# Decoder layer (linear mixer, cross-attention, expert-choice FFN) on one core: struck-out logits in PSUM, regrouped weight loads in the last batch, a ninth ring slot, first expert ahead of the bias work

## What is computed

```python
x = x + mixer(layernorm(x))                      # linear attention with running sums
Q = layernorm(x) @ Wq.T; K, V = ctx @ Wkv.T      # ctx: (16, 750, 256), 16 heads of 32
x = x + softmax(Q K^T * scale) V @ Wo.T
# expert-choice FFN on xn = layernorm(x): 32 experts, each takes its best 8 tokens of 224
logits = xn @ gate_w.T + gate_b
probs = softmax(logits, axis=tokens)
vals, idx = top_k(probs per expert, 8)
merged = sum_k vals[k] * xn[idx[k]]              # one row per sequence and expert
h = gelu([merged, 1] @ w1[e]);  o = [h, 1] @ w2[e]
x = x + scatter_add(idx, o * vals)
```

## Time and profile before

| what | us |
|---|---|
| median of 3 runs | 2262.58 (2260.3 to 2263.67) |
| the profiled execution, its own time | 2257.76 |
| its span, first to last instruction | 2256.1 |
| attention stage ends, expert stage begins | about 1577 of the span |
| PE busy over the span | 1858.3 (82%) |
| DVE busy | 1028.3 (46%) |
| POOL busy | 823.6 (37%) |
| chain of work that ended last: transfers into the ring | 22% of the span |

### The profile page before, as it was taken

The page is one execution under the profiler, slowest core; times in us unless marked ns, Lnnn a source line. Parts: engine busy times, 40 slices in busy tenths (PEclk is TensorE's granted clock), DMA queues, the critical chain, the costliest instruction groups (busy, mean ns, idle before and its releaser), DMA issues. The chain is left out here.

```text
span 2256.1 us, 41492 instructions
## 1 busy us (share of the span) xinstructions
PE 1858.3 (82%) x12594; PEld 1211.7 (54%) x12594; DVE 1028.3 (46%) x2541; ACT 745.9 (33%) x1551; POOL 823.6 (37%) x591
## 2 busy tenths in 40 slices
PE   7889999999999999999999999976756656556544
PEld 5667777677677776777777777753211111111111
DVE  1355766667667666666676666642100000000003
ACT  3144444445445444454454543532100000000000
POOL 0255555545555555465555555543000000000000
PEclk9799999999999999999999999977878787787776
DMA  5324333333243243332432433364899999999996
GB/s 172 88 67 109 78 77 95 82 87 95 74 106 77 76 97 81 89 96 74 103 78 76 99 80 82 80 223 146 367 418 421 421 420 423 422 420 421 422 377 252
DMA packets 143265, 421.34 MB, mean 187 GB/s; under 512 B 33036, under 2 KB 79084, under 8 KB 118652
## 3 DMA queue, kind: packets, MB, share of 16 engines
q1 hardware_dynamic: 135580, 411.70, 53.4%
q10 hardware_dynamic: 6656, 8.15, 1.0%
q0 software_dynamic: 992, 1.02, 0.1%
HBM read 307.37 MB, written 17.14 MB: 144 GB/s over the span
## 5 line engine op out<-in xcount | busy, mean ns | idle before, releaser
L1139 DVE TENSOR_REDUCE maxes<-bank 112x1 f32<-112x376 f32 (+1 forms) x1024 | 511.1, 537 | 129.6 <-PE bank L1345 127.0
L943 ACT ACTIVATE probs<-bank 125x448 f32<-125x448 f32 x768 | 399.5, 546 | 156.9 <-PE bank L1367 150.0
L1367 PE MATMUL bank<-q_st,k_st 98*125 98x224 f32 x1536 | 338.6, 307 | 23.5 <-DMA q_st<-max_lo 21.9
L821 POOL TENSOR_TENSOR psum_keys<-psum_keys,probs 125x896 f32<-125x896 f32 x127 | 266.6, 2099 | 214.9 <-ACT probs L943 209.8
L1345 PE MATMUL bank<-k_st,q_st 96*112 96x376 f32 (+1 forms) x1024 | 319.6, 358 | 21.5 <-DVE maxes L1139 18.9
L1753 PE MATMUL bank<-ring,hid_T 128*32 128x512 f32 x1024 | 175.5, 848 | 194.2 <-DMA ring<-in_L_ffn_w 191.0
L1367 PEld LDWEIGHTS bank<-q_st,k_st 98*125 98x125 f32 x1536 | 258.3, 192 | 82.2 <-issue 48.1
L1671 DVE TENSOR_TENSOR o_fin<-bank,b_row 16x512 f32<-16x512 f32 x32 | 21.7, 679 | 586.0 <-PE bank L1711 586.0
L824 POOL TENSOR_TENSOR psum_keys<-psum_keys,probs 125x896 f32<-125x896 f32 x127 | 266.7, 2100 | 9.9
L1593 POOL DMA_DIRECT2D o_rows<-o_fin x31 | 15.2, 492 | 597.7 <-DVE o_fin L1671 597.7
L1345 PEld LDWEIGHTS bank<-k_st,q_st 96*112 96x112 f32 x1024 | 170.2, 181 | 77.9 <-DVE maxes L1139 50.3
(11 more groups left out here) (168 smaller groups left out, 2762.4 us busy)
## 6 DMA issues: line engine op xcount, KB each, us to landing
ring<-in_L_ffn_w SPq DMA_DIRECT2D x128, 2048.0 KB, 30.4
k_st<-k_hi SPq DMA_DIRECT2D x512, 93.8 KB, 2.1
k_st<-k_lo SPq DMA_DIRECT2D x256, 93.8 KB, 2.2
q_st<-q_hi SPq DMA_DIRECT2D x504, 28.0 KB, 1.8
ctx_nat<-in_ctx SPq DMA_DIRECT2D x16, 750.0 KB
x_in<-in_x SPq DMA_DIRECT2D x16, 448.0 KB, 3.7
out<-x SPq DMA_DIRECT2D x16, 448.0 KB, 3.1
out<-ring ACTq DMA_DIRECT2D x28, 256.0 KB, 3.0
```

Source lines behind the costliest of these rows:

```text
L821: nc.gpsimd.tensor_tensor(psum_keys[:], psum_keys[:], lo, ALU.add).then_inc(pool_chain, 1)
L943: nc.scalar.activation(probs[n % 2][:, j, :], bank[5 + u % 2][0:SK, 0:2 * T], ACT.Exp, scale=SCALE).then_inc(probs_ready, 1)
L1139: nc.vector.tensor_reduce(maxes[:, j, t, c:c + 1], score_bank(n)[0:TT, 0:SC[c + 1] - SC[c]], AX.X, ALU.max).then_inc(s_drained, 1)
L1367: last = nc.tensor.matmul(bank[5 + u % 2][0:SK, kk * T:(kk + 1) * T], k_st[slot][:, j, k * SK:(k + 1) * SK], q_st[slot][:, j, :], start=Tr ...
```

## The change

- `beaten` lies in PSUM, in the unused half of the bank that holds the gate logits of that batch. `z_mix` is left to the mixer.
- The ring has nine places. Four tensors that were elsewhere (`wv_lo`, `ctx_lo`, `xh`, `bias_row`) and a rest now fill the place of the ninth, number 4 (`EXTRA`); the former slots 4 to 7 sit one place further (`home_of`). After the mixer's last use, chunk 0 of expert 2 is loaded into it once and read from there by `expert(1, 0, False, EXTRA)`; the first round of reloads leaves that chunk out. The expert loops start at 2, with round 1 written out.
- In the last batch the eight first chunks are released at the start of a group: each group's first `scores_T` must be done, then chunks 0, 1, 2 (group 0), 3, 4 (group 1), 5 and the extra one (group 2), 6 (group 3), and 7 after the last scores. `store` now comes behind the first three; `keep_weight` and `keep_routed` come behind chunk 6.
- `tok` is cleared at the start of the attention stage. The first expert's w1 matmuls come before PE's transposes of the bias rows, and DVE does both `take` of round 0 before `adder` and `b1_T`.

```diff
+        EXTRA = 4
+        def home_of(slot):
+            return slot if slot < EXTRA else slot + 1
...
-        wv_lo = sb(es, "wv_lo", [P, KC, D], F32R)
-            bias_row = sb(es, "bias_row", [TT, D])
+        tok = sb(es, "tok", [P, 2, KD, 32])
...
+        wv_lo = inside("wv_lo", P, [KC, D], F32R)
+        ctx_lo = inside("ctx_lo", P, [KC, S], F32R)
+        xh = inside("xh", TT, [2, D])
+        bias_row = inside("bias_row", TT, [D])
         end_slot()
...
-        ring = sb(es, "ring", [P, SLOTS, 2 * H])
+        ring = sb(es, "ring", [P, SLOTS + 1, 2 * H])
...
+                def extra_weight():
+                    sp.wait_ge(yt_ready, 2 * B)
+                    sp.wait_ge(x_bias_ready, B)
+                    sp.wait_ge(chunk_in[0], 16)
+                    load_chunk(sp, 2, 0, None, 0)
+                def last_batch_weights(kt):
+                    if kt == 0:
+                        sp.wait_ge(x1_ready, 2 * B)
+                        first_weights([0])
+                        sp.wait_ge(v_ready, NK * B)
+                        sp.wait_ge(q_ready, 4 * B)
+                        sp.wait_ge(k_ready, 8 * B)
+                        first_weights([1, 2])
+                    elif kt == 1:
+                        sp.wait_ge(q_stacked[3], 192 * B)
+                        sp.wait_ge(k_stacked[3], 192 * B)
+                        first_weights([3, 4])
+                    elif kt == 2:
+                        first_weights([5])
+                        extra_weight()
+                    else:
+                        first_weights([6])
...
+                        if kind == "last":
+                            sp.wait_ge(scores_ready, (LAST * 4 + kt) * 12 + 1)
+                            last_batch_weights(kt)
                         if kt == 3 and kind != "first":
                             keep_weight(b - 1)
...
                     nc.gpsimd.memset(weight[:], 0.0).then_inc(constants, 1)
+                    nc.gpsimd.memset(tok[:], 0.0).then_inc(cleared, 1)
...
+                def beaten(kind):
+                    return bank_of("gate", kind)[0:E, T:2 * T]
...
-                    nc.vector.match_replace(beaten[:], top8[:], logits[:], NEG
+                    nc.vector.match_replace(beaten(kind), top8[:], logits[:], NEG
                                             ).then_inc(router_chain, 1)
...
-                    nc.vector.scalar_tensor_tensor(out=weight[0:E, :], in0=beaten[:], scalar=NEG,
+                    nc.vector.scalar_tensor_tensor(out=weight[0:E, :], in0=beaten(kind), scalar=NEG,
...
-                with sp.Fori(1, E // 2 - 1) as i:
+                weights(1, 0, False, (1, 2, 3))
+                weights(1, 1, False)
+                with sp.Fori(2, E // 2 - 1) as i:
...
+                        slot = home_of(slot)
+                        if extra is not None and kd < 2:
+                            slot = extra
...
                     last.then_inc(h_full, 1)
+                    if first and e2 == 0:
+                        flip_biases()
...
                 expert(0, 0, True)
                 expert(0, 1, True)
-                with pe.Fori(1, E // 2) as i:
+                expert(1, 0, False, EXTRA)
+                expert(1, 1, False)
+                with pe.Fori(2, E // 2) as i:
```

More of the change, by code:

```diff
@@ L109, in build @@
     assert N_MID % 2 == 0
+    assert all(q.index("wt0") - q.index("gate") <= 2 for q in (SEQ["mid"], SEQ["last"], SEQ["tail"]))
     def place(job, kind):
@@ L1674, in _ @@
                 take(0, 0, True)
+                take(0, 1, True)
+                for c in range(HC):
+                    part = slice(c * 32, (c + 1) * 32)
+                    nc.vector.tensor_copy(adder[part, :], ident[part, part]
+                                          ).then_inc(adder_ready, 1)
+                dve.wait_ge(b1_flipped, 1)
+                nc.vector.tensor_copy(b1_T[:].rearrange("p t c e -> p (t c e)"), bank[4][:]
+                                      ).then_inc(b1_ready, 1)
                 add_biases(0, 0, True)
-                take(0, 1, True)
                 row_out(0, 0, True)
```

74 lines of the change are left out of this document (26 added, 48 removed).

## The result

The changed kernel takes 2235.72 us (median of 4 runs, 2233.17 to 2237.96), the kernel before beside it 2262.26: ratio 0.9883, interval 0.9866 to 0.99. It is faster by 26.5 us; I had said 16.4, and a time of 2246.2 in a range from 2237. Timed again in another comparison it was 2240.91 against 2258.9, ratio 0.9922 (0.9904 to 0.9939), 18.0 us. Its profiled execution took 2234.32 us (span 2232.7), 23.4 us less than that of before.

A forecast was written before the change was run, and what follows sets the result against it. Weight stream bounds the expert stage; in attention PE is fullest, and its last-ending waits matter. Gains 9.4 + 1.4 + 1.0 + 4.6 = 16.4 us take the profiled 2257.76 to 2241.4; adding 4.8 gives 2246.2, range 2237 to 2257.

The forecast's parts named there:

- Struck-out logits in PSUM: Router's third group: instruction shortens to 0.39 us, wait at wt0 goes; 0.67 us a batch, 9.4 us over fourteen middle batches.
- that now hangs on the PE score matmul of 532.51: Router's third group: q_lo waits on this matmul through DVE's preceding maximum, so wt1 moves only from 534.17 to 533.50.
- the bound of 1.5 us a batch: Middle batches: upper bound of the PSUM edit's gain, all of what DVE gains; lower bound nothing.
- Rival 1: Middle batches: another wait fills the gap at wt0, or PSUM does not free the instruction; 2257.0 us, chance 0.12.
- rival 4: Router: striking out into PSUM is much slower; at 1.90 us an instruction the kernel takes 2269.3 us, chance 0.03.
- Last batch: Last attention batch: 1.4 us gained from the PSUM edit and 1.0 us from the release by groups.
- rivals 2 and 3: Last batch: max rows come out between chunks, 2238.5 us, chance 0.12; or wait for everything issued before, 2252.2, chance 0.10.
- they land 1 us earlier: Last batch: with the store behind the first chunks, max rows still wait about one chunk but land 1 us earlier.
- Ninth slot and first expert: Expert stage: one chunk of 5.0 us fewer, PE starts 1.8 us earlier, stream gap of 2.2 us; gain 4.6 us.
- the port rule: Expert stage start: whichever POOL instruction or two-port DVE copy starts first holds shared ports throughout; sum 0.4 us smaller.
- the first term: Middle batches: gain from striking out logits into PSUM, 0.67 us a batch, 9.4 us.
- the third term: Expert stage: gain from the ninth slot and the earlier first expert, 4.6 us, bounds 3 and 7.5.

The follow-up runs named there:

- run 1: Kernel before with only the struck-out logits moved to PSUM; 18.5 us faster than the kernel before, ratio 0.9915.
- run 3: Changed kernel with the last batch's chunks issued at the places of the kernel before; 2242.44 us.
- run 6: Changed kernel, but each last-batch group's chunks are issued only after that group's max rows have landed; 10.4 us faster than the changed kernel beside it.
- run 7: Changed kernel with the last store and the recall of routed rows issued ahead of chunk 7; 5.9 us faster than the changed kernel.
- run 11: Changed kernel with max rows ahead of the weights, last store ahead of chunk 7 and picks cleared late; 2226.32 us.
- runs 6 and 12: The second of these: run 11 plus a second chunk issued to fill the expert stage's stream gap, against the changed kernel; 2223.23 us.

## Why the prediction was right and wrong

*Struck-out logits in PSUM.* That PSUM frees the instruction, and that PE's wait at wt0 goes with it, was right; what PE waits for next was wrong, and so the term was too small, 0.67 us a batch where 13 of the 14 batches gave 1.2: 9.4 us forecast, 14.9 measured, 14.3 alone. The step that failed is "that now hangs on the PE score matmul of 532.51, since DVE must first take the maximum of the one before it". These rows of before show what VectorE did behind the long instruction:

```profile
530.19 0.36 PE L1345 MATMUL bank<-k_st,q_st 96*112 96x376 f32 x1
...
532.81 0.53 DVE L1139 TENSOR_REDUCE maxes<-bank 112x1 f32<-112x376 f32 x1
```

The maximum of 532.81 was for the score matmul of 530.19, over since 530.55; it stood late only because VectorE was held. I tied it to the matmul just ahead of it in time, when it read an older one. In the changed kernel it runs at 529.42, more than 1 us ahead of the last score matmul, and q_lo no longer hangs on it: wt1's 0.29 us went as well. I had the bound of 1.5 us a batch on paper and took the nearest row's wait as the value; a count of maxima against score matmuls would have told. (A smaller slip: the earlier trace rows show 67 to 109 GB/s in slices 2 to 26, not 66 to 109 everywhere before the last quarter; nothing hung on it.) Rival 1 (the gap is filled) fell, and so did rival 4: 0.372 us into PSUM against 0.364, as small as taken.

*Last batch.* 2.4 us forecast (1.4 + 1.0), 5.4 measured, 4.6 over all executions of this form. The PSUM edit alone shortens it by 2.7, the release by 1.9 (from run 1) or 2.3 (from run 3) more. The picture of the release was right to the row: three chunks ahead of the store, both collisions kept. So rivals 2 and 3 fell. But the step "they land 1 us earlier" failed: the two collisions last 12.5 us in sum, against 12.2 before, and the forecast 1.0 us is not there. What the batch gained beyond the 1.4 us came from a term that I had put at nothing: at each collision the granted clock falls to 0.50, and how long it stays there differs (20 us before, 14 when the changed kernel was run again, 10 in its first execution and in run 6, 17 in run 7, at the first group). I had read the clock of 0.50 in the earlier trace rows and used it only for an idle window. The PSUM term has a part in it: in both kernels with the struck-out logits in SBUF, PE's wait of 1.48 us in the group of the earlier trace rows is followed by a stretch at the lower clock,

```profile
1526.00:1530.00 4.00, 2.99 (x25) 1.94 (x29) 2.44 (x6) 2.05 (x6) 3.38 (x3) 0.61 0.05 11
```

and from the weight transposes to the turning of the maxima PE took 3.9 us. In the changed kernel and in run 1 wait and stretch are gone, the clock is 1.00 there and the same work takes 2.7. So the edit is worth 1.2 us more than the 1.4 forecast, 2.6 in all, which is about what run 1 gained. For the release 0.5 to 2.3 us are left, by which kernel it is taken from; what of it is chance is open.

*Ninth slot and first expert.* 4.6 us forecast, 3.3 measured at first, 1.3 when the kernel was run again. The gap was right: 2.5 us were left of a chunk's 5.0, and 2.1 us came back when it was filled (584.1 to 582.4 and 581.6), for 2.2 forecast. PE's start too: 1.7 us sooner, 1.8 forecast; the copies were held until the clearing's end, about 1558.2, as the port rule of the Trainium skill has it that the prediction cites (SBUF — State Buffer, two separate sides); in time the 1.5 us from the stage's start lie between my 1.3 and the 1.7 by that rule. Two things took their share: w1 matmuls of 6.62 us instead of 5.90, at the lower clock (by chance, it seems: 4.94 when the kernel was run again), and a read-back that is on average 1.4 us longer in kernels with the slot. Why the read-back's rate differs is not settled.

*Total.* The forecast missed the first comparison by 10.5 us and the range by 1.3; 5.5 of it are the first term, 3.0 the last batch, the third term was 1.3 too large, and the remaining 3.3 are the distance of the profiled executions from the medians, 4.8 us in my sum and 1.4 in the changed kernel. The second comparison, 18.0 us, lies near the forecast, but not for its reasons: its middle batches gave the same 15 us.

## What to carry to other kernels

To price a shortened instruction, write down for each instruction queued behind it which producer it reads, not which one stands just ahead of it in time: work that was held up is often long ready, and then more than the next wait goes with it. A small transfer that an engine waits for goes out ahead of large ones or it waits for one of them; here moving the release behind two such transfers was worth more than the new release itself. Price a stretch at half clock as well as the stall ahead of it (run 11: some 3 us of a group of 17), and cut the span at fixed instructions before comparing two kernels, since their totals differ by 4 us from run to run.

## What the runs showed of the hardware

A VectorE instruction with two SBUF inputs takes 1.90 us beside a GpSimd sum and 0.36 alone; with one of them in PSUM it takes 0.38 at any moment. Two VectorE copies from late into tok, 1.35 us beside a clearing, take 0.36 ahead of it.

The max rows need 1.8 to 2.4 us with no chunk ahead of them (3.1 once, in run 11, 0.6 us behind the store) and 5.7 to 7.6 us behind chunks of 2048 KB, in all kernels without edit 6; 4.5 with 0.8 MB of chunks left (run 11). With three chunks issued ahead they do not wait for all of them: 2.9 of 6.3 MB were moved until they had landed. A lead of 0.3 us was enough to escape once (run 7).

TensorE fell to the lower clock in the last batch even where PE waited only 2.1 us (run 6), while in the middle batches, where PE has other work beside such a wait, it stays at 1.00. Behind a wait of 1.8 us it fell in runs 6 and 12 and not in run 11. At the first group it came back after 10 to 20 us, in run 7 after 16 us in which PE was busy throughout; what decides when was not tried. In the 24 us in which rows are read back from the output 276 to 327 GB/s were moved, at full share of the 16 engines, where the weights alone move 421.
